# Loading the second halves of x's first four tiles from GpSimd's queue instead of SyncE's

## The reference

```
logits = x @ Wr.T + 5 * one_hot(language of the row)           # 8 experts
gates  = softmax over the two largest logits, spread over the 8 experts
x1     = x + x @ W.T + 2 * sum_e gates_e * (x @ A_e.T) @ B_e.T  # W 1024 x 1024, A_e 16 x 1024
out    = x1 + x1 @ weight[adapter of the row].T                 # 8 of 16 matrices of 1024 x 1024
```

## Time and profile before

| what | value |
|---|---|
| device time, median of 3 | 396.9 us |
| device time of the profiled execution | 396.9 us |
| span of its trace | 395.1 us |
| granted TensorE clock | 1.00 |
| TensorE matmuls busy | 389.8 us, 99% |
| VectorE busy | 307.9 us, 78% |
| ScalarE busy | 173.8 us, 44% |
| GpSimd busy | 60.7 us, 15% |
| DMA moved | 68.60 MB, mean 174 GB/s |

### The profile page before, as it was taken

One profiled execution on the slowest core, in us unless ns is written; L12 is line 12 of the kernel. 1 busy time (PEld: TensorE's weight loads), 2 busy tenths in 40 slices (PEclk: granted clock), 3 DMA queues, 4 the chain that ended last, 5 costly groups with the idle time before them and its releaser, 6 DMA issues.

```text
span 395.1 us, 5948 instructions
## 1 busy us (share of the span) xinstructions
PE 389.8 (99%) x1888; PEld 329.9 (83%) x1888; DVE 307.9 (78%) x415; ACT 173.8 (44%) x245; POOL 60.7 (15%) x86
## 2 busy tenths in 40 slices
PE   8999999999999999999999999999999999999996
PEld 8888988888889888888888888888888888888886
DVE  3899998988554757048877967999999999999600
ACT  3362283554400243254275334555665656556411
POOL 3134300000000000000110211332321231312000
PEclk9999999999999999999999999999999999999999
DMA  7999750113776100009492999999999999897212
GB/s 202 226 224 216 109 147 2 53 55 107 234 217 165 25 1 0 2 1 247 130 330 71 274 265 273 274 253 278 259 280 291 286 267 302 256 268 166 80 53 55
DMA packets 88129, 68.60 MB, mean 174 GB/s; under 512 B 16386, under 2 KB 87074, under 8 KB 87586
## 3 DMA queue, kind: packets, MB, share of 16 engines
q1 hardware_dynamic: 61472, 46.59, 49.2%
q10 hardware_dynamic: 26626, 21.64, 17.9%
HBM read 53.51 MB, written 14.68 MB: 173 GB/s over the span
## 4 chain that ended last, share of the span: by engine, by line
PE 97%; DMA 1%; SPq 1%; issue 0%; DVE 0%; ACT 0%
PE banks L1421 15%; PE banks L1419 15%; PE banks L1420 15%; PE banks L1282 13%; PE banks L1284 13%; PE banks L1283 13%; PE banks L1275 6%; PE banks L1260 2%; PE banks L1296 2%; PE banks L1293 2%; PE banks L1295 2%; DMA sums<-in_L_cond_Wr_dram 1%; PE banks L1314 0%; SPq L436 0%; SPq L483 0%; SPq L429 0%
## 5 line engine op out<-in xcount | busy, mean ns | idle before, releaser
L1282 PE MATMUL banks<-ring,weights 128*128 128x512 f32 x192 | 75.2, 392 | 0.0
L1420 PE MATMUL banks<-weights,tokens 128*128 128x512 f32 (+1 forms) x184 | 69.9, 380 | 0.0
L1421 PE MATMUL banks<-weights,tokens 128*128 128x512 f32 (+1 forms) x184 | 69.9, 380 | 0.0
L1419 PE MATMUL banks<-weights,tokens 128*128 128x512 f32 (+1 forms) x184 | 69.9, 380 | 0.0
L1106 ACT ACTIVATE weights<-weights_f 128x1024 fp32r<-128x1024 f32 x44 | 46.6, 1061 | 50.1 <-DVE weights_f L759 49.3
L512 POOL TENSOR_TENSOR raw<-raw,ident 128x128 f32<-128x128 f32 x42 | 30.0, 714 | 219.2 <-DMA raw<-in_L_cond_weight_dram 219.1
L759 DVE STREAM_TRANSPOSE weights_f<-raw 128x1024 f32<-128x1024 f32 x42 | 51.7, 1232 | 8.2 <-POOL raw L512 7.7
L765 DVE TENSOR_TENSOR weights<-weights_f,weights 128x1024 fp32r<-128x1024 f32 x44 | 52.7, 1198 | 0.7 <-ACT weights L1106 0.6
L1284 PE MATMUL banks<-ring,turned_w 128*128 128x512 f32 x128 | 49.8, 389 | 0.0
L1283 PE MATMUL banks<-tokens,weights 128*128 128x512 f32 x128 | 49.8, 389 | 0.0
L1282 PEld LDWEIGHTS banks<-ring,weights 128*128 128x128 f32 x192 | 36.0, 188 | 7.6 <-issue 0.3
(11 more groups left out here) (131 smaller groups left out, 626.0 us busy)
## 6 DMA issues: line engine op xcount, KB each, us to landing
raw<-in_L_cond_weight_dram SPq DMA_DIRECT2D x168, 128.0 KB, 5.2
ring_f<-in_L_cond_weight_dram SPq DMA_DIRECT2D x88, 128.0 KB, 5.5
out_dram<-sums ACTq DMA_DIRECT2D x31, 256.0 KB, 5.6
raw<-in_x_dram SPq DMA_DIRECT2D x48, 128.0 KB, 3.3
x_kept<-stage ACTq DMA_DIRECT2D x24, 256.0 KB, 3.1
raw<-in_L_cond_W_dram SPq DMA_DIRECT2D x16, 128.0 KB, 3.4
turned_w_f<-in_x_dram SPq DMA_DIRECT2D x12, 128.0 KB, 3.4
ring_f<-in_L_cond_W_dram SPq DMA_DIRECT2D x12, 128.0 KB, 3.6
```

The lines of the kernel that those rows point to most:

```text
L1282: nc.tensor.matmul(ps, u_hi, x_hi, start=first and k == 0, stop=False, skip_group_check=True)
L1419: nc.tensor.matmul(ps, x_hi, w_hi, start=m == 0, stop=False)
L1420: nc.tensor.matmul(ps, x_hi, w_lo, start=False, stop=False)
L1421: mm = nc.tensor.matmul(ps, x_lo, w_hi, start=False, stop=m == M - 1)
```

## The change

GpSimd, right after its constants, waits until ScalarE has made the high part of x's tile 1, issues the four DMAs of the second halves of tiles 0 and 1, and then makes the low part of x's tile 1; it then waits for the high part of x's tile 3, issues the four DMAs of the second halves of tiles 2 and 3, and makes the low part of tile 2. SyncE no longer issues these eight DMAs. The helper `low` of GpSimd moves up unchanged.

```
@@ sync @@
             for r in range(1, HM):
                 fill(sp, W0_PLACES[r], w0_rows(r), w_loaded[r])
             fill_a_half(sp, 1)
-            fill_x(sp, 0, 1)
-            fill_x(sp, 1, 1)
             fill_w_half(sp, 1)
             for item in LOADS:
                 load(item)
@@ gpsimd @@
             nc.gpsimd.tensor_copy(iota_f[:], iota_i[:]).then_inc(setup, 1)
+            for pair in range(2):
+                pool.wait_ge(hi_done, PIECE_AT["xl", 2 * pair + 1] + 1)
+                fill_x(pool, pair, 1)
+                low(("xl", pair + 1))
...
-            low(("xl", 1))
-            low(("xl", 2))
             pool.wait_ge(diagonal, 3)
             low(("wr", 1))
```

More of the change, by code:

```diff
@@ L499, in _, with low @@
         def _(pool):
+            def low(p):
+                pool.wait_ge(hi_done, PIECE_AT[p] + 1)
+                src, high_part, low_part = sides(p)
+                nc.gpsimd.tensor_tensor(low_part, src, high_part.bitcast(F32), ALU.subtract).then_inc(pool_lo_done, 1)
             nc.gpsimd.memset(wr_raw, 0.0).then_inc(wr_zeroed, 1)
@@ L533, in make_s3 @@
                 nc.gpsimd.tensor_tensor(a11, a11, a21, ALU.subtract).then_inc(s3_done, 1)
[L535 to L543, removed]
             pool.wait_ge(diagonal, 3)
```

## The result

The changed kernel takes 414.95 us (414.36 to 415.24, five runs) against 396.9: the ratio is 1.0449, 95% interval 1.0436 to 1.0462. The forecast was 402.5 with a range of 398.0 to 406.5. The direction was right, the size was not: 18 us instead of 5.6. The profiled execution took 415.24 us, its span is 413.4.

What follows compares the result with a forecast made beforehand. TensorE bounds the kernel: its first feeding plus a stream of some 380 us. All terms were 0 but GpSimd's delay of product 1: span 395.1 + 5.6 = 400.7, and 1.8 around it, 402.5 us; range 398.0 to 406.5.

Steps and rivals of the forecast that it cites:

- What bounds the kernel: TensorE, busy 99%: its first feeding plus some 380 us of stream; a delay in the front is paid in full.
- Eight issues gone from SyncE, gain 0: SyncE's queue loses 4.83 us of issues; what stood behind goes up to 4.8 us earlier, nobody waited: 0.
- Earlier arrival, gain 0: x's second halves are requested earlier, but VectorE turns the last two at 23.14 without a wait: 0.
- The price of an issue, 1.28: Time g of one DMA issue on GpSimd, taken as 1.28 us; product 1 starts 5.6 us late, at 19.9.
- 8 g: Eight issues ahead of the end of GpSimd's second low part; product 1's delay is 8 g - 4.6 us.
- the 0.58 from which it would decide: The time of one GpSimd issue, in us, below which product 1 would not be delayed.
- Rival E: GpSimd can't write requests beside a dense VectorE; product 1 is 15.3 us late, 412.2 us; chance 0.04.
- W's tiles share the engines: Early x requests delay VectorE's low parts of W by up to 2.2 us, covered by the GpSimd wait: 0.
- the 1.30 against rival E: GpSimd's low part took 1.30 us beside a busy VectorE, 1.27 beside a less busy one; cited against that rival.
- The clock, rival B: TensorE's pause before product 1 drops its clock to the lower level: 1.5 to 3.0 us more, 404.0 to 405.5; chance 0.18.
- the forecast's own idle stretch of 5.4 us: TensorE idle before product 1, from 14.5 to 19.9, waiting for GpSimd's second low part.
- A: The forecast itself: product 1 waits for GpSimd, 5.6 us late, no fall of the clock, 402.5 us; chance 0.50.

Runs made afterwards that it cites:

- experiment 7: Changed kernel, scratch 3072 bytes, GpSimd issuing all eight DMAs only behind both low parts and the turning of W's tile 1: 400.72 us, ratio 1.0093.
- 8: As experiment 7, with SyncE also waiting, before the right half of W's tile 0, until W's tile 3 is turned: 398.09 us against 396.68, ratio 1.0032.
- experiment 1: Changed kernel with a descriptor scratch of 3072 bytes instead of 1024, B's low part written over its high part for room: 401.24 us against 397.09, ratio 1.0113.
- experiment 4: Changed kernel with the eight early DMAs issued by ScalarE's queue instead of GpSimd's, GpSimd's low parts as in the kernel before: 402.12 us, ratio 1.0125.
- experiment 6: Changed kernel, scratch 1024, with 60 or 68 extra identity matmuls on TensorE between first features and product 1: 416.38 us with 60, 414.90 with 68.

## Why the prediction was wrong

**What bounds the kernel: right.** No later wait took up the delay, and from product 1 on the changed kernel runs as before but for the clock.

**Eight issues gone from SyncE, gain 0: wrong in sign.** Their place in the queue had kept the next x tiles behind x's second halves. Where x's second halves were asked for at the old time, the freed queue cost 2.3 us (experiment 7 against 8). In the changed kernel itself this was not separated.

**Earlier arrival, gain 0: right.** In none of the runs did it give anything.

**The price of an issue, 1.28: the failed step, in two ways.** The term 8 g was too large: 0.59 measured, 4.8 us and not 10.2, almost at the 0.58 from which it would decide. By it alone product 1 would have started at 14.4. And the sum had no term for a wait inside the row of issues: the 15.1 us of pauses. Taking only durations of issues, on any engine, as the bounds of g ended the range at 6.6, and no row of the trace before could show the pauses, as GpSimd issued nothing there. But the code could have raised the question: the size of the scratch stands in the program's own call, and the range should have had a case for a GpSimd that must wait for its requests to be consumed. Rival E had a stall of that size by another mechanism: 15.3 us late against 15.5, for the wrong reason, and it had 0.04.

**W's tiles share the engines: right in kind, wrong as a cover.** I put VectorE's low parts up to 2.2 us later, under the wait for GpSimd. In the changed kernel that cover held, as TensorE waited for nothing else. Once the pauses are gone it is the bound. The runs lose 4.15 us (experiment 1) and 5.0 (experiment 4), but the waits behind W's late tiles are 1.8 and 3.9 of that, against an estimate of up to 2.0; most of the rest is VectorE's long instructions in the one and the clock in the other. The estimate let only the first four requests ahead of W's tiles. I take it that W's tile 3, for which VectorE waits 2.8 us in experiment 1, also met the second four; no run separates this. The sum had no term at all for VectorE's own instructions becoming longer beside GpSimd's issues: the 1.30 against rival E was read on GpSimd's side only.

**The clock, rival B: it happened.** I gave it 0.18 beside the forecast, at 1.5 to 3.0 us. It cost 2.8, and with 68 small matmuls ahead of it product 1 took 11.01 us again. By the rule of the Trainium skill ("TensorE: Matmul & The Clock Gate", section "Part 1: The HAM clock gate") an idle engine falls to the lower rate; here the granted clock shows it at 0.50. The clock fell also behind the waits of 3.2, 3.9, 4.2 and 6.3 us of other runs, and cost 1.9 to 2.7 us each time. So with the forecast's own idle stretch of 5.4 us, B should have weighed more than A. A length from which a wait does this can't be read off: one of 2.6 us did not (experiment 6), one of 2.4 did (experiment 7).

The 18.3 us of the span are then: pauses, issues and low parts ahead of product 1, 15.5, and the clock, 2.8. The changed kernel does not show what it would lose by W's late tiles alone, as that lies under the wait for GpSimd.

## What to carry to other kernels

Before DMA issues are moved to GpSimd, look at the descriptor scratch in the program's constructor and at what stands behind the issues on GpSimd: a full scratch turned a 0.59 us issue into a wait of 2.7 to 7.3 us that no semaphore shows, and it held up the compute instructions behind it too. And ask what TensorE's clock will do behind a wait: in six of these profiled executions it added 1.6 to 2.8 us to one. A single queue was here also an order of priority: requests moved to another queue competed with those that they used to follow, and the requests that they left behind competed with them. VectorE and TensorE had no wait on these transfers, and asking for them earlier only took from what was asked for at the same time.

## What the runs showed of the hardware that was not expected

- GpSimd's issue of this pattern (256 pieces of 512 bytes) takes 0.58 to 0.73 us, 0.45 on SyncE. Three go without a pause with a scratch of 1024 bytes, five with 1536, eight with 3072.
- The room is not given back as soon as the data have moved. These are the packets and MB of GpSimd's own queue, and its share of the time of the 16 DMA engines, in the changed kernel from 9 to 11, 11 to 13 and 13 to 15 us; the fourth issue came at 14.65.

```profile
q0 software_dynamic: 67, 0.20, 48.9%
...
q0 software_dynamic: 74, 0.19, 37.2%
...
q0 software_dynamic: 3, 0.00, 1.0%
```

The 0.39 MB of the first three requests had moved by about 13, and GpSimd stood for over a us more. The last pause of 6.9 us ended 1.3 us behind the last packet of the seventh request (at 26.5), although the fifth and sixth had moved by 22.7. Why it had to last that long is not explained, and neither is what GpSimd looks at to find room.
- At the start of every run TensorE's identity matmuls are slow for some 6 us with the granted clock at 1.00, while after the idle stretch the same slowness comes with 0.50 (0.42 us between matmuls of 512 columns against 0.23). The column does not tell of the first kind.
